# Turning the attention probabilities of rows 1 to 15: from TensorE to VectorE blocks and a round trip through device memory

## The reference, cut to what matters

```python
# attention block, per row
h = layernorm(layernorm(x)); q, k, v = split(h @ qkv_w + qkv_b)        # 16 heads of 16
attn = softmax(q . k[window of 15 neighbours] / 4)                      # radius 7
x1 = layernorm(x) + (attn . v) @ proj_w + proj_b
x  = x + x1 + gelu(layernorm(x1) @ fc1 + b) @ fc2 + b                   # hidden 1024
# feed-forward block, per row
z = layernorm(x)
e = top 2 of 8 experts by mean(z) @ w_gate
x = x + a * (gelu(z @ W1m) @ W2m) + (1 - a) * sum of the two gated experts (W1e, W2e gathered)
```

## Time and profile before

| | us |
|---|---|
| median of three runs | 1879.69 (1879.02 to 1880.44) |
| the profiled execution, its own time | 1879.39 |
| its span in the trace | 1877.6 |
| PE busy | 1865.5 (99%) |
| DVE busy | 1358.6 (72%) |
| ACT busy | 1169.2 (62%) |
| POOL busy | 872.1 (46%) |

### The profile page before, as it was taken

How to read it: one execution, slowest core, us unless ns; L and a number is a source line. 1 busy time by engine, 2 the same in 40 slices (tenths; PEclk the granted TensorE clock), 3 DMA queues, 4 the chain that set the end, 5 groups by cost and what they waited for, 6 DMA issues and landing times.

```text
span 1877.6 us, 49306 instructions
## 1 busy us (share of the span) xinstructions
PE 1865.5 (99%) x19591; PEld 1684.6 (90%) x19591; DVE 1358.6 (72%) x2230; ACT 1169.2 (62%) x1832; POOL 872.1 (46%) x788
## 2 busy tenths in 40 slices
PE   8999999999999999999999999999999999999999
PEld 7899898998989989899898999989899898998998
DVE  7776877778677686776867767687676877778644
ACT  5775755657566575665756657566575755657554
POOL 6545271543716436163462524536245271552725
PEclk9999999999999999999999999999999999999999
DMA  5230311203122031220313103131131311203121
GB/s 143 63 90 29 97 58 53 73 29 96 57 68 68 19 102 52 83 60 24 97 46 91 52 30 96 41 96 53 38 89 34 97 58 49 77 29 97 46 63 57
DMA packets 147438, 121.88 MB, mean 65 GB/s; under 512 B 17965, under 2 KB 140041, under 8 KB 147209
## 3 DMA queue, kind: packets, MB, share of 16 engines
q1 hardware_dynamic: 146512, 117.90, 21.9%
q10 hardware_dynamic: 696, 0.83, 0.2%
HBM read 85.52 MB, written 8.39 MB: 50 GB/s over the span
## 4 chain that ended last, share of the span: by engine, by line
PE 97%; DVE 1%; DMA 1%; ACT 0%; POOL 0%; issue 0%; ACTq 0%; DVEq 0%; POOLq 0%
PE psB L253 58%; PE psA L253 28%; PE psA L1266 4%; PE psA L1283 3%; PE psA L1155 2%; PE psA L1305 2%; PE psA L1321 0%; DMA raw<-in_L_attn_qkv_w 0%; DMA raw<-in_L_attn_fc_w 0%; DVE smax L726 0%; POOL y L520 0%; DMA xin<-in_L_attn_x 0%; PE psB L1340 0%; ACT y L1019 0%; DVE pr L743 0%
## 5 line engine op out<-in xcount | busy, mean ns | idle before, releaser
L626 DVE TENSOR_TENSOR hr_lo<-hf,hr_hi 128x512 fp32r<-128x512 f32 x512 | 495.5, 968 | 435.8 <-ACT hr_hi L982 435.8
L514 POOL TENSOR_SCALAR wx_hi<-raw 128x512 fp32r<-128x512 f32 x256 | 196.6, 768 | 658.6 <-DMA raw<-in_L_ffn_W2e 387.7
L982 ACT ACTIVATE hr_hi<-hf 128x512 fp32r<-128x512 f32 x512 | 324.2, 633 | 276.0 <-PE psB L253 187.9
L516 POOL TENSOR_TENSOR wx_lo<-raw,wx_hi 128x512 fp32r<-128x512 f32 x256 | 410.8, 1605 | 21.4
L978 ACT ACTIVATE hf<-psB,b1x 128x512 f32<-128x512 f32 x256 | 175.4, 685 | 178.2 <-PE psB L253 177.0
L253 PE MATMUL psB<-wx_hi,hr_hi 128*128 128x256 f32 x1016 | 285.2, 281 | 0.2
L253 PE MATMUL psB<-wx_hi,hr_lo 128*128 128x256 f32 x1016 | 284.1, 280 | 0.0
L253 PE MATMUL psB<-wx_lo,hr_hi 128*128 128x256 f32 x1016 | 283.5, 279 | 0.0
L253 PE MATMUL psB<-z_hi,wx_hi 128*128 128x512 f32 x512 | 211.8, 414 | 0.0
L253 PE MATMUL psB<-z_hi,wx_lo 128*128 128x512 f32 x512 | 202.5, 396 | 0.0
L253 PE MATMUL psB<-z_lo,wx_hi 128*128 128x512 f32 x512 | 201.1, 393 | 0.0
(11 more groups left out here) (213 smaller groups left out, 4643.9 us busy)
## 6 DMA issues: line engine op xcount, KB each, us to landing
raw<-in_L_ffn_W1e SPq DMA_DIRECT2D x256, 128.0 KB, 2.2
raw<-in_L_ffn_W2e SPq DMA_DIRECT2D x256, 128.0 KB, 2.2
vb<-vs SPq DMA_DIRECT2D x64, 192.0 KB
vb<-vs SPq DMA_DIRECT2D x64, 160.0 KB
out_x<-acc SPq DMA_DIRECT2D x31, 256.0 KB, 2.2
xin<-in_L_attn_x SPq DMA_DIRECT2D x15, 512.0 KB, 3.7
tm<-in_L_ffn_b2e SPq DMA_DIRECT2D x32, 128.0 KB, 3.0
raw<-in_L_attn_fc_w SPq DMA_DIRECT2D x8, 256.0 KB, 3.5
```

What stands on the lines that cost most here:

```text
L514: g.tensor_scalar(wx[0][:, s, :], raw[:, s, :], 1.0, 0.0, ALU.mult, ALU.add).then_inc(w_hi.sem, 1)
L516: g.tensor_tensor(wx[1][:, s, :], raw[:, s, :], wx[0][:, s, :].bitcast(f32), ALU.subtract).then_inc(w_lo.sem, 1)
L626: v.tensor_tensor(hr[1][:, c % 2, :], hf[:, c % 3, :], hr[0][:, c % 2, :].bitcast(f32), ALU.subtract).then_inc(h_lo.sem, 1)
L982: a.activation(hr[0][:, c % 2, :], hf[:, c % 3, :], ACT.Copy).then_inc(h_hi.sem, 1)
```

## The change

For rows 1 to 15 the turning of the probabilities is done in another way; row 0 keeps TensorE's (`turn_first`, `turned_first`).

- VectorE's `turn_blocks(t, u)` follows each `normalise(t, u)`: one instruction of 128x768 that transposes 32x32 blocks. `blocks(u)` is its destination: the tiles `y` (unit 0), a new tile `blk` (1 and 2), `sx` (3).
- SP's `place_turned(t, u)` stores this to a scratch tensor `turned` in device memory (384 KB, pieces of 1 KB), waits until that has landed, and loads it in three transfers of 128 KB, each to 32 partitions. `attend` waits for the three. `PLACED` says where in SP's program: unit 0 ahead of the load of expert chunk 5, unit 1 ahead of chunk 6, units 2 and 3 ahead of chunk 8.
- The queries of unit 2 are laid out by ScalarE at step 3 (`query_blocks_first`) and no more by VectorE.
- ScalarE's `norm1_y` goes from step 5 to step 6 and also waits for the store of unit 0 (which reads `y`); GpSimd's `norm1_bias` goes from step 7 to 8; VectorE's `attended_low(t, 1)` from step 12 to 13.
- The padding goes: a group has 48 keys, a turned unit and `vb` have 96 partitions, `zT` has no border, and the memsets of the padding at the start of the kernel go (9 on VectorE become 2, a 32x4096 one on GpSimd goes).

```diff
+        PLACED = {RING + 1: (0,), RING + 2: (1,), 2 * RING: (2, 3)}
...
+            def place_turned(t, u):
+                sp.wait_ge(blk_s.sem, blk_s.at(t - 1, u))
+                if u == 0:
+                    sp.wait_ge(t1_lo.sem, t1_lo.all(t))
+                    sp.wait_ge(av.sem, av.all(t - 1))
+                elif u == 1 and t > 1:
+                    sp.wait_ge(store.sem, store.all(t - 2))
+                elif u == 2:
+                    sp.wait_ge(av.sem, av.at(t, 1))
+                sp.dma_start(turned[u, :, :, :].rearrange("c p n -> p c n"), blocks(u).rearrange("p c b k -> p c (b k)")).then_inc(blk_out.sem, 16)
+                sp.wait_ge(blk_out.sem, blk_out.at(t - 1, u))
+                for c in range(PB):
+                    dst = turned_flat(t, u)[SQ * c:SQ * c + SQ, :].rearrange("p (s n) -> p s n", s=HS)
+                    sp.dma_start(dst, turned[u, c, :, :].rearrange("(s k) n -> k s n", k=SQ)).then_inc(pT_in[u].sem, 16)
...
+                            if t < ROWS and n in PLACED:
+                                for u in PLACED[n]:
+                                    place_turned(t, u)
                             if n >= RING:
                                 sp.wait_ge(w_hi.sem, w_hi.at(f, n - RING))
...
-                    elif q == 7 and t:
+                    elif q == 8 and t:
                         norm1_bias(t)
...
+            def turn_blocks(t, u):
+                v.wait_ge(normed.sem, normed.at(t, u))
+                if u == 0:
+                    v.wait_ge(sx_s.sem, sx_s.at(t - 1))
+                elif u == 1 and t > 1:
+                    v.wait_ge(blk_out.sem, blk_out.at(t - 2, 2))
+                elif u == 2:
+                    v.wait_ge(blk_out.sem, blk_out.at(t - 1, 1))
+                elif u == 3:
+                    v.wait_ge(acc_s.sem, acc_s.at(t - 1, 1))
+                src = pr[:, (u % 2) * UW:(u % 2 + 1) * UW].rearrange("p (b c k) -> p c b k", c=PB, k=SQ)
+                v.transpose(blocks(u), src).then_inc(blk_s.sem, 1)
...
                         if q == 3:
                             normalise(t, 0)
+                            if t:
+                                turn_blocks(t, 0)
                         elif q == 9:
                             normalise(t, 3)
+                            if t:
+                                turn_blocks(t, 3)
...
-                        if t:
-                            query_blocks(t, 2)
...
                     elif q == 4 and t > 0 and t < ROWS:
                         normalise(t, 1)
+                        turn_blocks(t, 1)
...
                         normalise(t, 2)
+                        if t:
+                            turn_blocks(t, 2)
...
-                    elif q == 12 and t < ROWS:
+                    elif q == (13 if t else 12) and t < ROWS:
                         attended_low(t, 1)
...
             def norm1_y(t):
                 if t:
                     a.wait_ge(sx_s.sem, sx_s.at(t - 1))
+                    a.wait_ge(blk_out.sem, blk_out.at(t - 1, 0))
...
                     elif q == 3 and t:
                         keys(t, 1)
+                        query_blocks_first(t, 1)
...
-                    elif q == 5 and t:
+                    elif q == 6 and t:
                         norm1_y(t)
...
             def attend(t, u):
...
+                if t:
+                    pe.wait_ge(pT_in[u].sem, pT_in[u].all(t - 1))
```

More of the change, by code:

```diff
@@ L535, in _ @@
             g.wait_ge(hbias_s.sem, KD)
[L536 to L543, removed]
+            for s, i in ((0, 0), (HS - 1, NT - 1)):
+                g.memset(vb[:, s, i, :], 0.0).then_inc(zeroed.sem, 1)
             roots(0, *EXTRA[0])
@@ L790, in norm1_z @@
                 v.wait_ge(rstd[0].sem, rstd[0].at(row - 1))
-                v.wait_ge(av.sem, av.all(row - 1))
+                if row > 1:
+                    v.wait_ge(av.sem, av.all(row - 1))
+                else:
+                    v.wait_ge(trp.sem, trp.all(0))
                 for i in range(NT):
@@ L1164, in chunk_up @@
                 else:
-                    ps, z, off = psB, z3, 0
+                    ps, z = psB, z3
                     w1, _ = chunk_weights(m)
@@ L1179, in chunk_up @@
                         pe.wait_ge(t2_lo.sem, t2_lo.at(t, k))
-                    last = three(pe, ps[:, m % 2, :], w1[k], [a[:, k, off:off + T] for a in z], k == 0, k == KD - 1)
+                    last = three(pe, ps[:, m % 2, :], w1[k], [a[:, k, :] for a in z], k == 0, k == KD - 1)
                 last.then_inc(up.sem, 1)
@@ L1220, in project_qk @@
                         pe.wait_ge(t1_lo.sem, t1_lo.at(t, k))
-                    last = three(pe, psA[:, bank, :], [w[:, k, col:col + P] for w in wqkv], [z[:, k, LEFT:LEFT + T] for z in zT], k == 0, k == KD - 1)
+                    last = three(pe, psA[:, bank, :], [w[:, k, col:col + P] for w in wqkv], [z[:, k, :] for z in zT], k == 0, k == KD - 1)
                 last.then_inc(qk.sem, 1)
@@ L1304, in attend @@
                             w = (HS * c + s) * G * HD
-                            last = pe.matmul(psA[cols, 2 + c, at:at + QB], vb[0:PK, j, 2 * th + h, w:w + G * HD], turned_unit(t, u)[0:PK, b, cols], start=True, stop=True)
+                            last = pe.matmul(psA[cols, 2 + c, at:at + QB], vb[:, j, 2 * th + h, w:w + G * HD], turned_block(t, u, b, s), start=True, stop=True)
                     last.then_inc(av.sem, 1)
@@ L1312, in project @@
                         for k in parts:
-                            last = three(pe, proj_bank(t, h)[:, j * D:(j + 1) * D], [z[:, k, LEFT + i * P:LEFT + (i + 1) * P] for z in zT],
+                            last = three(pe, proj_bank(t, h)[:, j * D:(j + 1) * D], [z[:, k, i * P:(i + 1) * P] for z in zT],
                                          [w[:, k, :] for w in wproj], k == 0 and j == 0, k == KD - 1 and j == 1)
```

194 lines of the change are left out of this document (96 added, 98 removed).

## The result

| | us |
|---|---|
| before, median on the same chips | 1879.71 |
| after, median of 4 runs | 1944.0 (1940.65 to 1951.37) |
| ratio | 1.0347, 95% interval 1.0324 to 1.0369 |
| the profiled execution after, its own time and its span | 1943.58, 1941.9 |

The change is slower by 64 us; the prediction said 9 faster. The page of the kernel after answers to the earlier trace rows: TensorE is busy for 96% instead of 99%, with 480 transposes fewer.

The account below looks back on a forecast made before the run. TensorE, busy 99%, was taken to bound the kernel: 3.52 us a row saved, all but 0.6 lost to waits, so fifteen rows gain 9 us: 1870.5 us, likeliest range 1861 to 1875.6, overall 1858 to 1902.

Parts of the forecast that it names:

- with all cover intact 1826.6: Whole kernel: if TensorE gets no new waits, losing its transposes in rows 1 to 15 saves 52.8 us from 1879.4.
- one wait at step 11: TensorE waits 2.8 us a row for VectorE's low half of chunk 9, losing what three of four transpose groups gave.
- the chain of steps 8 and 9: VectorE's gapless low halves, normalises and gather plus two block transposes of 0.95 us; low half 9 ends at 469.1 to 469.5.
- a placing is 6.0 us: On SP, one unit's store, landing, three loads and their landing, with wakes, take 6.0 us, bounds 5.5 to 7.9.
- a wait of 0.9, which costs nothing: TensorE waits 0.9 us before `attend` of unit 1, at no cost since step 11 waits longer.
- rival 1: SP's queue delays unit 1 before `attend`; at a placing of 7.0 us a row loses 1.5, 1902 us; chance 0.27.
- break-even of 6.5: On SP, a placing of about 6.5 us would cancel the gain; above it the forecast's sign is wrong.
- The prediction's other sign of being wrong: At ScalarE's `norm1_y`, moved to step 6: a wait there for unit 0's store would show the forecast wrong; 0.7 us slack.
- Rival 2: Block transposes on VectorE take 1.74 us each in steps 8 and 9; a row loses 1.0, 1895 us; chance 0.10.
- X: VectorE's block transpose of 128x768: taken as 0.95 us, bounds 0.92 to 1.74.
- rival 4: VectorE and ScalarE have room, so TensorE's waits do not come: much faster, 1826.6 us; chance 0.06.
- rival 3: A draw: a placing on SP takes 6.5 us, gain and waits cancel, 1876 to 1883 us; chance 0.12.

Follow-up runs that it names:

- e2: The changed kernel without the store and loads, each block transpose replaced by a one-column memset, so nothing is turned in rows 1 to 15: 1871.83 us, ratio 0.9961.
- e8: e5 with GpSimd's `norm1_bias` at step 12 instead of step 8: 1856.8 us, ratio 0.9876.
- e6: The kernel before with one unused tile of 32 bytes a partition ahead of `zT`: 1895.68 us, ratio 1.0085.
- e5: e2 with one unused tile of 32 bytes a partition ahead of `zT`: 1867.29 us, ratio 0.9934.
- e1: The changed kernel without the store and the three loads; `attend` waits for VectorE's block transpose alone: 1918.87 us, ratio 1.0205.
- e7: The changed kernel with e3's store order, e5's 32 bytes, `norm1_bias` at step 12, `normalise(t, 3)` behind low half 9, `attend(t, 3)` at step 13: 1890.89 us.
- e3: The changed kernel with SP issuing the stores of units 0 and 1 one behind the other, then the loads: 1924.79 us, ratio 1.0243.
- e4: The changed kernel with twelve idle 128x512 matmuls ahead of the wait of `attend(t, 1)`: 1931.55 us, ratio 1.0275.

## Why the prediction was wrong

**The steps that were right.** The block transpose took 0.98 us where 0.95 was taken. The estimate of 0.8 from the Trainium skill's "Vector Engine (DVE) Microarchitecture Reference", section "The reshape front-end and per-opcode configuration", was near. The 1.9, an estimate worked out from the Trainium skill's "VectorE: DVE Perf Modes", section "The three transpose paths", was twice too much; the 311 ns there are for bf16, and the tiles here are float32. What the same page advises in its section "Rules for kernel authors", TensorE where PSUM will do, fits these runs: no kernel with all four units turned on VectorE was faster than the kernel before. The transposes' own 0.88 us were right as well: the turning's 44.2 us in 14 rows are gone. In row 4 the first store went out 0.35 us behind the forecast (460.36 less 11.21 against 448.8). The forecast's last addition, 1870.4 and 0.3, makes 1870.7 and not 1870.5, which changes nothing.

**Step 1 that failed: "with all cover intact 1826.6", less one wait at step 11.** e2 has nothing of what was added and takes 1872. TensorE, earlier by a group of transposes at each of four steps, meets the low half of chunk 6 before it is ready (9 us in 15 rows), the gather at step 10 (4 us) and the low half of chunk 9 (12 us), the first because `norm1_bias` runs beside it (e8). Another 17 us are the 256-column products. That a move of tiles in SBUF slows them is shown by e6 in the kernel before, and e5 takes back half of it with 32 bytes; that all of the 17 is from there is inferred. The prediction cost "the padding goes" at nothing, and the low half of chunk 6 at nothing.

**Step 2: the chain of steps 8 and 9.** Its wait was put at 2.8 us; e1 has 2.0 in row 4. But it comes on top of the others, as TensorE reaches step 11 later than thought. Counted from the row's start, low half 8 was put at 34.2, behind a ScalarE that is 1.5 us earlier, and came at 35.2; VectorE has no idle time ahead of it, in e2 neither, so it was VectorE's own work, with the two stretched low halves in it, that set the start of the chain. The blocks of unit 3 were put at 42.3 and done at 43.5 (475.70 less 432.21); and low half 9 behind them took 1.44 us, beside GpSimd's split, not 0.7: 44.8 instead of 43.0 to 43.4. The dependence of chunk 8's `chunk_down` on the first gather (16.3 us in e1, 21.7 in e7) wasn't in the prediction. Together the block transposes cost 47 us, with some 8 of half clock at step 12 among them.

**Step 3: "a placing is 6.0 us", and "a wait of 0.9, which costs nothing".** Unit 1's took 7.4 us in row 4 (466.58 to 473.98), inside its bounds of 5.5 to 7.9: the store 2.9, not 2.6, from the first to the last issue of the loads 0.9, the last load some 3.6, not 2.2. Unit 0's store took 3.6, not 2.6, and as SP waits for it unit 1's store went out 1.4 late. By the formula of the Trainium skill's "DMA: Bandwidth & Descriptors", section "Anatomy of one DMA — SWDGE (gpsimd) path", which was fitted to transfers that GpSimd issues, a store is 2.9 and a load 2.3, as an estimate. The medians here, of transfers that SP issues, are near: 2.8 for all 60 stores and 2.5 for the loads. The forecast's terms were too short. The wait became 2.24 us in row 4 and 3.0 on average (45.2 / 15). It does cost, and not as the prediction had it: VectorE's gather waits for the `chunk_down` that stands behind `attend` (the 1.86 us at 478.43, 29.1 in the whole kernel against 2.5 in e1 and e3), so the chain of step 9 starts later. This was rival 1's mechanism, at a placing of 7.0 and 1902 us. It was right in kind and named a break-even of 6.5; alone it accounts for 25 us of the 64. The prediction's other sign of being wrong, ScalarE waiting for the store in `norm1_y`, came too: 9.1 us in 10 times. What it costs was not measured apart; e3 has nearly as much of it (8.6 us), so it is not what e3 gave back.

**Step 4, in no part of the prediction: the clock.** Behind the longest waits the matmuls come at half speed: 17 us at step 9 in the kernel after, of which e4 gives back 12.5 net. They are no term beside the 25 us of step 3 but lie within them, since in e1 and e3 step 9 is as fast as before. e1 and e3 have their own slow stretches, at step 12.

So the sum: 1826.6, + 17 slower products, + 28 waits that are there with nothing turned (25 of them found at steps 8, 10 and 11), + 47 block transposes, + 25 transfers = 1944. Rival 2 is out, as X was right; so is rival 4, since even the kernel with no turning had no room for 1826.6; rival 3's placing of 6.5 was too short as well. The forecast's fault was to treat the deepest wait as the only one. What stays open is by what rule the places in SBUF set the matmuls' speed, and why a wait of 2.0 us is followed by the half clock in some rows and not in others.

## What to carry to other kernels

When work is taken from the engine that bounds a kernel, everything it reads must come earlier by as much. List, for each step behind the first saving, what that step waits for and its slack, not only the deepest wait; an empty waits view says nothing of slack. Take away all of the added work in one experiment first: here the empty shell alone had lost 45 of 53 us, and until that is mended no better place for the additions could bring more than the other 8. And a long wait hides a later one only in part if it is upstream of it: here the wait for the transfer took 48 us and the half clock behind it 17, while the steps behind became some 40 shorter. Look whether the engine that ends the second wait itself waits for the engine that stands at the first.

## What the runs showed of the hardware

- An unused tile of 32 bytes a partition ahead of others slowed the kernel before by 0.85% (interval 0.68 to 1.02%), one of 64 bytes by 0.63%: weight loads of 190 instead of 188 ns and twelve matmuls of 256 columns 1.435 instead of 1.406 us with the 32 bytes. A change of a tile's size is no neutral edit here.
- Around and behind a wait of 4.3 us TensorE's granted clock was 0.53 and 0.62 in two windows of 4 us; twelve idle matmuls ahead of the wait, in every row, gave back 12.5 us.
- A 0.69 us subtraction on VectorE took 1.4 to 1.8 us where it ran beside GpSimd's elementwise work, in the kernel before too; here the slack of such instructions should have been counted at the long figure. VectorE's and GpSimd's timelines of the kernel before, row 4:

```profile
453.79 1.79 DVE L626 TENSOR_TENSOR hr_lo<-hf,hr_hi 128x512 fp32r<-128x512 f32 x1
456.80 1.56 DVE L626 TENSOR_TENSOR hr_lo<-hf,hr_hi 128x512 fp32r<-128x512 f32 x1 [1.22 <-ACT hr_hi L982]
```
```profile
454.99 2.82 POOL L520 TENSOR_TENSOR y<-y,bproj 128x1024 f32<-128x1024 f32 x1
```

- SP issued a store in 0.38 us and each of its loads in 0.43; the landing of 384 KB in device memory took 2.5 us at best, 2.8 in the median and 5.4 at worst.
